# A wait at the end of each edge batch: GpSimd holds until the batch's last scatter has landed

## The reference

```python
xl = (x @ Wl).reshape(n, H, D)           # H = 4 heads of 64
xr = (x @ Wr).reshape(n, H, D)
msg = xl[src] + xr[dst]                  # one row for each edge
act = jnp.where(msg > 0, msg, NEG_SLOPE * msg)
e = jnp.einsum('ehd,hd->eh', act, att)   # 4 scores for each edge
m = jax.ops.segment_max(e, dst, num_segments=n)
...
out = jax.ops.segment_sum(alpha[..., None] * xl[src], dst, num_segments=n)
```

## Time and profile before

| | us |
|---|---|
| runs, median (lowest to highest) | 3107.69 (3086.83 to 3109.86), 3 runs |
| the profiled execution: its span, the only time that is given of it | 3314.6 |
| PE busy in it | 2750.0 (83%) |
| DVE busy | 1628.8 (49%) |
| ACT busy | 949.5 (29%) |
| POOL busy | 801.2 (24%) |

### The profile page before, as it was taken

The page is one execution under the profiler, slowest core; times in us unless marked ns, Lnnn a source line. Parts: engine busy times, 40 slices in busy tenths (PEclk is TensorE's granted clock), DMA queues, the critical chain, the costliest instruction groups (busy, mean ns, idle before and its releaser), DMA issues. The chain is left out here.

```text
span 3314.6 us, 51753 instructions
## 1 busy us (share of the span) xinstructions
PE 2750.0 (83%) x19258; PEld 2574.3 (78%) x19258; DVE 1628.8 (49%) x3236; ACT 949.5 (29%) x1933; POOL 801.2 (24%) x790
## 2 busy tenths in 40 slices
PE   3676677688887959968996899989999999999368
PEld 3544477687877958957885799989999989999257
DVE  6365545465556257765553622225545432226445
ACT  3254432222222034513442210023433211001033
POOL 0254556545455113312221000000000000000244
PEclk7788788788898968867998899999999999999589
DMA  9742232222226298525774511111112455124163
GB/s 224 194 121 64 78 99 83 73 76 80 74 69 184 79 228 205 136 82 138 204 204 95 149 44 42 31 48 54 52 30 79 111 168 136 58 65 122 31 233 136
DMA packets 221773, 362.95 MB, mean 110 GB/s; under 512 B 38358, under 2 KB 164950, under 8 KB 220299
## 3 DMA queue, kind: packets, MB, share of 16 engines
q1 hardware_dynamic: 185117, 278.93, 29.6%
q0 software_dynamic: 36432, 80.98, 9.5%
HBM read 272.99 MB, written 98.18 MB: 112 GB/s over the span
## 5 line engine op out<-in xcount | busy, mean ns | idle before, releaser
L317 PE MATMUL mix_bank<-mix_wkv_hi,layer_act_hi 128*125 128x256 f32 x1280 | 366.6, 286 | 18.4 <-issue 18.1
L319 PE MATMUL mix_bank<-mix_wkv_hi,layer_act_lo 128*125 128x256 f32 x1280 | 366.1, 286 | 18.8 <-issue 18.5
L318 PE MATMUL mix_bank<-mix_wkv_lo,layer_act_hi 128*125 128x256 f32 x1280 | 365.7, 286 | 13.0 <-issue 12.7
L525 POOL DMA_INDIRECT edge_gl<-xl,edge_idx x168 | 170.3, 1014 | 394.1 <-DVE edge_e L591 227.3
L318 PEld LDWEIGHTS mix_bank<-mix_wkv_lo,layer_act_hi 128*125 128x125 f32 x1280 | 243.8, 190 | 22.0 <-issue 21.6
L319 PEld LDWEIGHTS mix_bank<-mix_wkv_hi,layer_act_lo 128*125 128x125 f32 x1280 | 243.4, 190 | 20.1 <-issue 20.0
L317 PEld LDWEIGHTS mix_bank<-mix_wkv_hi,layer_act_hi 128*125 128x125 f32 x1280 | 243.6, 190 | 19.3 <-issue 17.9
L844 PE MATMUL count_pa<-count_hot_s,count_hot_d 125*125 125x416 bf16 (+1 forms) x624 | 153.5, 413 | 79.2 <-DVE count_hot_s L758 59.1
L532 POOL DMA_INDIRECT scores<-edge_e,edge_idx x168 | 177.0, 1054 | 131.0 <-DMA scores<-edge_e,edge_idx 83.4
L844 PEld LDWEIGHTS count_pa<-count_hot_s,count_hot_d 125*125 125x125 bf16 x624 | 101.1, 168 | 132.2 <-DVE count_hot_s L758 70.4
L317 PE MATMUL out_bank<-out_w_hi,layer_act_hi 128*125 128x256 f32 x640 | 187.6, 293 | 11.8 <-DVE layer_act_lo L1911 6.3
(11 more groups left out here) (554 smaller groups left out, 7619.0 us busy)
## 6 DMA issues: line engine op xcount, KB each, us to landing
ffn_raw<-in_L_ffn_w_dram SPq DMA_DIRECT2D x16, 2048.0 KB
scores<-targets_hole SPq DMA_DIRECT2D x40, 546.9 KB
gat_sc<-scores SPq DMA_DIRECT2D x10, 2187.5 KB
ffn_raw<-in_L_ffn_W_dram SPq DMA_DIRECT2D x16, 1024.0 KB
mix_raw<-in_L_mix_w_qkv_dram SPq DMA_DIRECT2D x24, 512.0 KB
sage_cnt<-at SPq DMA_DIRECT2D x20, 546.9 KB
layer_slab<-in_L_gnn_W_neigh_dram SPq DMA_DIRECT2D x8, 1024.0 KB
layer_slab<-in_L_gnn_W_self_dram SPq DMA_DIRECT2D x8, 1024.0 KB
```

The source lines that it names most:

```text
L317: pe.matmul(out, lhs[0], rhs[0], start=first, stop=False)
L318: pe.matmul(out, lhs[0], rhs[1], start=False, stop=False)
L319: return pe.matmul(out, lhs[1], rhs[0], start=False, stop=last)
L525: pool.indirect_dma_start(buf[:, slot, j, :], None, x, self.at(row, EB * b + j)).then_inc(self.s_g[slot], 16)
```

## The change

After the gathers and scatters of a batch GpSimd waits until the last scatter of that batch has landed. Batches that issue no scatter (0 to 7) have no such wait; the other 76 have one. The value waited for is the one that line 531 waits for ahead of the next scatter. No instruction is added, removed or moved besides this wait.

```diff
@@ Edges.gpsimd
             for d in done[1:]:
                 for j in range(EB):
                     self.scatter(pool, d, j)
+            if done:
+                pool.wait_ge(self.s_sc, 16 * (T + 1) + 16 * EB * done.stop)
         if end == BATCHES:
```

## The result

The changed kernel takes 3171.1 us (median of 4 runs, 3167.1 to 3176.3), the kernel before 3105.0 us beside it (4 runs, 3086.8 to 3109.9): a ratio of 1.0215, 95% interval 1.0187 to 1.0242, slower by 66 us. The forecast was 3186 us and slower by 78. Measured again in 6 more runs, the whole change came to a ratio of 1.0243 (1.0214 to 1.0273). The recorded span fell all the same, from 3314.6 to 3171.7 us. Of the 83 timed executions of the kernel before in this study 82 took 3082 to 3127 us and one 8894, which the ratios leave out; none lies near 3315.

What follows compares the result with a forecast made beforehand. Unrecorded, POOL was taken as nearly level with PE in the mix block and its bound once waits are added. Mix 68, count 4 and output 6 sum to +78 us on 3107.7, giving 3186; range 3080 to 3225.

Steps and rivals of the forecast that it cites:

- The first reading: Mix block: PE's recorded stalls come from being recorded; without them the block takes 433 us instead of 575.
- POOL's own work: Mix block: 120.7 us for batches 24 to 31, then 7.66 us for each of the other 40.
- 6 us of room in 433: Mix block: POOL would end at 855 against PE's 861, nearly level with it.
- The price of a wait: Each added wait adds 1.62 us after an ordinary batch and 1.11 after one with four scatters.
- Mix: Mix block: 48 added waits make POOL the bound, +68 us, between 0 and +108.
- Count: Count block: 16 added waits, partly absorbed by POOL's wait for DVE, some +4 us, between 0 and 26.
- Output: Output block: 12 added waits, partly hidden beside PE's later end, +6 us, between 0 and +18.
- A: Rival, chiefly mix block: PE's stalls are in every run and the wait thins them, 3033 us; chance 0.17.
- B: Rival: POOL's batches fit PE's pace, hiding the waits; +4 from the count block alone, 3112 us; chance 0.21 together with C.
- milder form: Mix block: POOL issues faster unrecorded, a batch with its wait takes 8.2 us under 8.7, nearly all hidden.
- C: Rival: the scatter has always landed by its batch's end, so nothing changes, 3108 us; chance 0.21 together with B.
- The mark that the forecast named: Whole kernel: the recorded span may fall, to about 3255 us, while the unrecorded time rises.

Runs made afterwards that it cites:

- again: The kernel before, unchanged, recorded and timed a second time: median 3104.2 us, ratio 1.0005.
- half_w: The added wait on a kernel before that issues only each batch's second-column scatter, leaving half of the scores unwritten: 3091.3 us, ratio 0.9955 against the kernel before.
- il: The kernel before, no added wait, with one gather between any two scatters of the batches with four: 3088.4 us, ratio 0.9944.
- w_each: The changed kernel with the wait after the first column's scatters too, so GpSimd waits twice a batch: 3306.0 us, ratio 1.0642 against the kernel before.

## Why the prediction was right, point by point

**The first reading holds in its result and not in its reason.** The forecast took the stalls of the earlier trace rows for "a cost of being recorded". They aren't: `again` is recorded too and has none, nor has any of the twelve other recordings, by the pauses of PE without a wait (88.2 us against 0.0). They belonged to that one execution. What was right was not to add up in a recording 207 us above the median, and to take PE's length from its undisturbed slabs: PE's need was put at 433 us, and in `again` its last matmul ends 427 us after the block's first instruction (784.4 - 357.1). The rule of the Trainium skill (NOTIFIC — the notification-queue block, section 7.1), which was given as support, is not borne out: thirteen recordings show no pause of PE of this kind, and for the one that does no row shows the notification block at work.

**POOL's own work was sized too low.** The forecast took the best stretch, 7.66 us for a batch. Over batches 32 to 71 `again` has 8.18, some 20 us more in all. About half of it is that an issue takes 1.3 to 1.5 us instead of 1.0 now and then, and the other half that a scatter is sometimes late: 12.1 of the 41.5 us of waits for scatters lie in these batches, the others in batches 24 to 31, which the forecast had measured as a whole. That measurement was off the other way, since a row was misread: 548.78 in the earlier trace rows is the second gather of batch 32, and its first is this:

```profile
544.92 0.99 POOL L525 DMA_INDIRECT edge_gl<-xl,edge_idx  x1 [0.30 <-issue]
```

So batches 24 to 31 took 116.8 us and not 120.7, and 116.0 in `again`; rightly read, the forecast's own rows would have given +64 for mix. POOL's last scatter ends 443 us into the block, not 427, and before the next block can start there come 4.92 us more:

```profile
799.11 1.00 POOL L532 DMA_INDIRECT scores<-edge_e,edge_idx  x1 [0.30 <-issue]
805.03 0.52 POOL L1883 MEMSET out_nil<- 128x512 bf16 x1 [4.92 <-POOLq L68]
```

So where the forecast had "6 us of room in 433", POOL was 16 us over PE (800.1 against 784.4) before the change. That alone would have made the change dearer than forecast.

**The price of a wait.** 1.62 us was taken, for 1.92 us of idle time after an ordinary batch. The wait is as bare as expected but shorter: of the 39 ahead of batches 33 to 71, 24 took 1.39 to 1.41 us, although each stood behind a scatter with gathers in front of it. So that isn't what made the 1.92 of the earlier trace rows; what did isn't shown. Over batches 33 to 71 the mean time ahead of a first gather rises from 0.30 to 1.73 us, by 1.43. But a batch grows only from 8.18 to 9.36 us, by 1.18. The difference comes back in POOL's other waits: those of the scatters for a late landing fall from 41.5 to 29.9 us in the block (from 12.1 to 3.2 in batches 32 to 71), since a scatter that was waited for at the batch's end can't be late later. The forecast left this out.

**Mix: +68 forecast, +51 to +54 measured.** The errors work against each other: no room was left to use up, and the wait was cheaper. The block's length came out at 501.6 us against 501 forecast, but that is partly luck: POOL's last scatter ends at 495 us instead of 501, and 6.2 us come on top before the next block starts, of which the sum had only the last batch's landing.

**Count: +4 forecast, +14 to +17 by the blocks.** This is the term that was mis-sized. The 4 us rested on DVE holding POOL back until 403 us. In `again` PE and DVE of this block end 19 us before it does, and POOL waits for DVE only 7.6 us from 180 on; the disturbed recording had 77.9. Hence the 16 waits cost about 1.0 us each. Nor did the last batch's wait vanish before the barrier, as the forecast had it: the 7.26 us there became 8.56. The upper bound of 26 us in the forecast was the right place to look.

**Output: +6 forecast, 0 by the blocks, +2.5 by the median.** The room was there, as the lower bound had it: POOL's last scatter in `again` ends 15 us before PE's last matmul (927.7 and 942.4).

**The sum** is 63 to 68 us by the blocks (882.3 and 887.0 less 819.3) and 66 to 75 by the runs; 78 was forecast. That it came so near is in part luck: mix was 14 to 17 us too high, output 6, and count 10 to 13 too low. **The rivals:** A (real stalls, 3033 us) falls with `again`, and with the time that rose. B (hidden) falls in the full kernel, but `half_w` shows that it would be right with 1.3 us less of scatter per batch. Its milder form (POOL issues faster unrecorded) has nothing for it. C falls with the 79.4 us of waits. The mark that the forecast named, a shorter span beside a longer time, came true, but it proved only that the first recording was long.

## What to carry to other kernels

Look for the engine that works alone at a block's end before judging an added wait, and then for its waits for other engines earlier in the block. Where it had hardly any, 79 us of added waits cost 51 to 54; where PE ended the block, 93 us cost 2.5; and where POOL ended it but had waited 36 us for DVE, 19.5 us cost nothing. If the recorded span doesn't agree with the median of the runs, record once more before building on its waits: here that would have shown at once that GpSimd ends two of the blocks. A landing that two other issues would have covered added 1.4 us of idle time in the mean when it was waited for bare and made a batch 1.2 us longer, and with one issue between two dependent scatters (`il`) most of such waits were gone.

## What the runs showed of the hardware

- A gather or a scatter takes GpSimd 0.95 to 1.0 us to issue, but some take 1.3 to 1.5 with nothing waited for. The mean in the mix block was 1.02 us.
- The bare landing of a scatter of 128 times 16 bytes took 1.40 us of idle time in 28 of 46 waits of the mix block, once a batch (mean 1.73), and a median of 1.87 ahead of a batch's first gather when every scatter was waited for.
- Between the end of GpSimd's last indirect DMA and its first instruction in the next block lie 4.9 us at the end of the mix block and 7.3 at the end of the count block (`again`), and 6.2 and 8.6 in the change, whose last wait lies in them. GpSimd, which ends these blocks, ends them that much later than the last row of its timeline seems to say. What fills this time isn't shown.
- PE's mean granted clock in the mix block was 0.97 before (`again`), 0.93 in the change and 0.87 in `w_each`, where the same 3072 matmuls stood in 448, 502 and 590 us; their busy time rose with it from 420 to 431 and 452 us, more of them having run at the lower of the two levels (1.2 and 2.4 GHz). PE's last matmul ended 21, 40 and 46 us before the block in the three, so nothing shows that this lengthened it.
